# Third norm's centred values in the first tile's banks, its stages and GpSimd's first work in another order, first layer's weights in two transfers

## The reference

```
x = x + mamba_both_ways(layernorm(layernorm(x)))     # 8 passes: 4 sequences, forwards and backwards, 16 states
x = x + ffn_ref(layernorm(x), ...)                   # the transformer; this layernorm is "the third norm"

ffn_ref(x): for i in range(6):
    x = attn_layer(shift_tokens(x), Wqkv[i], q_scale[i], k_scale[i], Wo[i]) + x     # 16 heads of 64, window 32
    x = ffn_layer(shift_tokens(x), ln_g[i], ln_b[i], W1[i], b1[i], W2[i], b2[i]) + x
layernorm(x) = (x - mean(x)) / sqrt(var(x) + 1e-5)   # over the 128 features
```

## Time and profile before

| | us |
|---|---|
| median of 3 runs | 3966.04 (3959.29 to 3967.46) |
| the profiled execution, its own time | 3973.11 |
| its span, first to last instruction | 3971.3 |
| PE busy in it | 3732.7 (94%) |
| DVE, POOL, ACT busy | 3320.7, 3235.6, 2912.0 |

### The profile page before, as it was taken

One profiled execution on the slowest core, in us unless ns is written; L12 is line 12 of the kernel. 1 busy time (PEld: TensorE's weight loads), 2 busy tenths in 40 slices (PEclk: granted clock), 3 DMA queues, 4 the chain that ended last, 5 costly groups with the idle time before them and its releaser, 6 DMA issues.

```text
span 3971.3 us, 110564 instructions
## 1 busy us (share of the span) xinstructions
PE 3732.7 (94%) x43392; PEld 2529.3 (64%) x43392; DVE 3320.7 (84%) x3407; ACT 2912.0 (73%) x6890; POOL 3235.6 (81%) x2370
## 2 busy tenths in 40 slices
PE   7999999997579999999999999999999999999997
PEld 2333333333267777777777777777777777777775
DVE  4999999999478887888878888788878888788885
ACT  6555545553268887888878888788878888788885
POOL 3888788888388888888888888888888888888883
PEclk8999998899789999999999999999999999999999
DMA  1222222222100000000000000000000000000001
GB/s 66 79 70 71 77 70 70 75 73 82 46 5 13 2 16 2 17 2 16 2 2 17 2 16 2 6 13 2 16 2 6 13 2 16 2 6 2 2 2 44
DMA packets 30703, 102.12 MB, mean 26 GB/s; under 512 B 4580, under 2 KB 6504, under 8 KB 29296
## 3 DMA queue, kind: packets, MB, share of 16 engines
q1 hardware_dynamic: 30192, 95.05, 7.0%
HBM read 90.32 MB, written 4.72 MB: 24 GB/s over the span
## 4 chain that ended last, share of the span: by engine, by line
PE 67%; issue 2%; ACT 1%; POOL 1%; DVE 0%; POOLq 0%; ACTq 0%; DVEq 0%
PE ps L1101 17%; PE ps L1029 13%; PE ps L1090 9%; PE ps L1040 8%; PE ps L1078 7%; PE ps L1126 5%; PE ps L1139 3%; PE ps L1063 1%; PE ps L1051 1%; PE ps L1108 1%; PE ps L1114 1%; ACT prob L1232 0%; PE ps L1011 0%; ACT mixed L1241 0%; POOL resid L1530 0%
## 5 line engine op out<-in xcount | busy, mean ns | idle before, releaser
L1508 POOL TENSOR_TENSOR resid<-resid,sq 128x1024 f32<-128x1024 f32 x384 | 910.3, 2376 | 3.9 <-DVE sq L1362 3.7
L626 POOL TENSOR_TENSOR read<-state,c_row 128x1024 f32<-128x1024 f32 x256 | 714.9, 2811 | 165.6 <-DVE state L588 85.7
L1530 POOL TENSOR_TENSOR resid<-resid,rnorm 128x1024 f32<-128x1024 f32 x384 | 725.0, 1904 | 18.1 <-POOL rnorm L1522 0.4
L1101 PE MATMUL ps<-mixed,w_vo 128*128 128x128 f32 x6144 | 720.2, 276 | 3.0 <-ACT mixed L1241 2.3
L1101 PEld LDWEIGHTS ps<-mixed,w_vo 128*128 128x128 f32 x6144 | 711.1, 192 | 13.0 <-issue 4.6
L1029 PE MATMUL ps<-w_qk,xs_parts 128*128 128x512 f32 x2304 | 640.3, 414 | 43.6 <-issue 18.7
L1232 ACT ACTIVATE prob<-ps,stat 128x64 f32<-128x64 f32 x3072 | 650.9, 383 | 0.3
L1362 DVE TENSOR_TENSOR sq<-ps,rope_l 128x1024 f32<-128x1024 f32 x384 | 462.5, 1205 | 104.7 <-ACT sq L1194 104.7
L393 PE MATMUL mamba_ps<-read,ident 128*128 128x512 f32 x1024 | 520.8, 652 | 14.8 <-POOL read L626 14.8
L1375 DVE TENSOR_TENSOR resid<-ps,rope_l 128x1024 f32<-128x1024 f32 x384 | 464.4, 1209 | 69.4 <-ACT sq L1194 62.3
L1029 PEld LDWEIGHTS ps<-w_qk,xs_parts 128*128 128x128 f32 x2304 | 415.8, 192 | 157.9 <-issue 81.7
(11 more groups left out here) (138 smaller groups left out, 5685.9 us busy)
## 6 DMA issues: line engine op xcount, KB each, us to landing
c_row<-c_rows SPq DMA_DIRECT2D x128, 512.0 KB, 3.6
w_stage<-w_qk_hbm SPq DMA_DIRECT2D x6, 1024.0 KB, 4.8
vo_stage<-w_v_hbm SPq DMA_DIRECT2D x6, 512.0 KB, 3.8
vo_stage<-w_o_hbm SPq DMA_DIRECT2D x6, 512.0 KB, 4.6
xn<-x_hbm SPq DMA_DIRECT2D x4, 512.0 KB, 7.0
kept<-resid SPq DMA_DIRECT2D x8, 256.0 KB, 4.5
resid<-kept SPq DMA_DIRECT2D x8, 256.0 KB, 4.4
out_hbm<-resid SPq DMA_DIRECT2D x8, 256.0 KB, 2.0
```

Of the source, the lines that this page charges most:

```text
L626: pool.tensor_tensor(read[:, h, g % 2, :], state[:, h, g % 2, :], c_row[:, g % C_AHEAD, :], ALU.mult).then_inc(done[f"rd{h}"], 1)
L1101: last = pe.matmul(bank[:, 0:P], w_vo[:, l % 2, head_at(place_h), :], mixed[:, odd, place_h, :], start=place_h == 0, stop=place_h == HEADS ...
L1508: pool.tensor_tensor(qk[:, tile % 2, cols], qk[:, tile % 2, cols], sq[:, 1 + part, :], ALU.add).then_inc(done[f"rotated{part}"], 1)
L1530: pool.tensor_tensor(heads, heads, norms, ALU.mult).then_inc(done[f"normed{part}"], 1)
```

## The change

Four things are altered.

The centred values leave the ring: chunks 0 to 3 go to banks 0 to 3, chunks 4 to 7 to banks 2 and 3 by turns (`in_bank`). Chunk c of 4 and more waits until `in_norm` of chunk c-2 is done. `project0` of tile 0 waits for chunks 0 and 1 to have left banks 0 and 1, `score` of tile 0 for all eight chunks.

The norm's stages have another order: chunks 4 to 7 come between the first two tiles' stages, and so do the folds. GpSimd makes both rotary tables first, and `low_qk1` after the first tile's `rest`.

PE and ACT no longer wait for DVE's constants at the block's start. GpSimd no longer waits for the small attention masks (`const_loaded`); the tables' transfer now counts on `scale_loaded`.

Each layer's queries' and keys' weights come in two transfers of 512 KB, one for each half, with a semaphore each.

The diff, cut to what does something:

```diff
--- before.py
+++ after.py
@@ -745,8 +745,7 @@
-TURN_READERS = {"in_centre": "in_norm", "in_variance": "in_log",
-                "head_turn0": "copy_heads0", "head_turn1": "copy_heads1", "head_turn2": "copy_heads2",
+TURN_READERS = {"in_variance": "in_rstd", "head_turn0": "copy_heads0", "head_turn1": "copy_heads1", "head_turn2": "copy_heads2",
...
-def staggered(*stages):
-
-    return [(name, i - behind) for i in range(CHUNKS + 1) for name, behind in stages if 0 <= i - behind < CHUNKS]
...
-    pe[0:0] = staggered(("in_centre", 0), ("in_variance", 1)) + [("fold0", 0), ("fold1", 0)]
-    act_in = staggered(("in_square", 0), ("in_log", 1), ("in_rstd", 1))
-    insert_after(act_in, ("in_rstd", 3), ("high_qk0", 0))
-    insert_after(act_in, ("in_rstd", 5), ("high_qk1", 0))
-    act[0:0] = act_in + [("copy_folded0", 0), ("copy_folded1", 0)]
-    dve[0:0] = [("in_norm", c) for c in range(CHUNKS)]
-    pool[0:0] = [("rope0", 0), ("low_qk0", 0), ("rope1", 0), ("low_qk1", 0)]
+    def norms(*stages):
+        return [(f"in_{name}", c) for name, c in stages]
+
+    pe[0:0] = norms(("centre", 0), ("centre", 1), ("variance", 0), ("centre", 2), ("variance", 1), ("centre", 3),
+                    ("variance", 2), ("variance", 3), ("centre", 4), ("centre", 5))
+    act[0:0] = norms(("square", 0), ("square", 1), ("log", 0), ("rstd", 0), ("square", 2), ("log", 1), ("rstd", 1), ("square", 3),
+                     ("log", 2), ("rstd", 2)) + [("high_qk0", 0)] + norms(("log", 3), ("rstd", 3)) + [("high_qk1", 0)]
+    dve[0:0] = norms(*[("norm", c) for c in range(4)])
+    insert_after(pe, ("project0", 0), *norms(("variance", 4), ("variance", 5)))
+    insert_after(pe, ("project1", 0), *norms(("centre", 6), ("centre", 7)))
+    insert_after(pe, ("project0", 1), *norms(("variance", 6), ("variance", 7)), ("fold0", 0), ("fold1", 0))
+    insert_after(act, ("round", 0), *norms(("square", 4), ("square", 5)))
+    insert_after(act, ("square0", 0), *norms(("log", 4), ("rstd", 4), ("log", 5), ("rstd", 5)))
+    insert_after(act, ("square1", 0), *norms(("square", 6), ("square", 7)))
+    insert_after(act, ("square0", 1), *norms(("log", 6), ("rstd", 6), ("log", 7), ("rstd", 7)), ("copy_folded0", 0), ("copy_folded1", 0))
+    insert_after(dve, ("squares0", 0), *norms(("norm", 4), ("norm", 5)))
+    insert_after(dve, ("squares0", 1), *norms(("norm", 6), ("norm", 7)))
+    pool[0:0] = [("rope0", 0), ("rope1", 0), ("low_qk0", 0)]
+    insert_after(pool, ("rest", 0), ("low_qk1", 0))
...
-    done |= {name: sem(name) for name in ("in_centre", "in_square", "in_variance", "in_log", "in_rstd")}
+    done |= {name: sem(name) for name in ("in_centre", "in_square", "in_variance", "in_rstd")}
-    names = """wqk_loaded wvo_loaded w1_loaded w2_loaded scale_loaded const_loaded const_set vo_folded vo_copied rope_ready partner_ready
+    wqk_loaded = [sem(f"wqk_loaded{part}") for part in range(2)]
...
+
+    def in_bank(chunk):
+
+        return ps[:, chunk if chunk < 4 else S + chunk % 2, :]
...
             def load_qk(l):
                 if l:
                     sp.wait_ge(w1_low, l)
-                sp.dma_start(w_stage[:, :], hbm["w_qk"][l]).then_inc(wqk_loaded, 16)
+                for part in range(2):
+                    cols = slice(part * INNER, (part + 1) * INNER)
+                    sp.dma_start(w_stage[:, cols], hbm["w_qk"][l][:, cols]).then_inc(wqk_loaded[part], 16)
...
             load_heads(0)
-            sp.dma_start(rope[:, :, :, :], hbm["rope"]).then_inc(const_loaded, 16)
+            sp.dma_start(rope[:, :, :, :], hbm["rope"]).then_inc(scale_loaded, 16)
             load_qk(0)
...
         @block.tensor
         def _(pe):
-            pe.wait_ge(const_set, CONSTS_SET)
-
             def in_centre(chunk):
-                bank = turn_free("in_centre", chunk)
-                pe.matmul(bank, centring[:, :], resid[:, chunk * BANK:(chunk + 1) * BANK], start=True, stop=True
+                if chunk >= 4:
+                    pe.wait_ge(x_ready, chunk - 1)
+                pe.matmul(in_bank(chunk), centring[:, :], resid[:, chunk * BANK:(chunk + 1) * BANK], start=True, stop=True
                           ).then_inc(done["in_centre"], 1)
...
-                elif last and last[0] == "in_centre":
-                    pe.wait_ge(x_ready, last[1] + 1)
...
+                elif last and last[0] == "in_variance":
+                    pe.wait_ge(done["in_rstd"], 2 * last[1] + 1)
...
@@ -1019,6 +1031,8 @@
                     after(pe, ("rest", tile))
                     if t == 0:
                         pe.wait_ge(wqk_low, 2 * l + part + 1)
+                    if tile == 0:
+                        pe.wait_ge(x_ready, 2)
...
-                    pe.wait_ge(const_loaded, 80)
+                    pe.wait_ge(const_loaded, 64)
+                    pe.wait_ge(x_ready, CHUNKS)
...
         @block.scalar
         def _(act):
-            act.wait_ge(const_set, CONSTS_SET)
             act.preload_act_table_set("natural_log_exp_and_others")
...
             def high_qk(part):
                 def stage(l):
                     cols = slice(part * INNER, (part + 1) * INNER)
-                    act.wait_ge(wqk_loaded, 16 * l + 16)
+                    act.wait_ge(wqk_loaded[part], 16 * l + 16)
...
             def in_square(chunk):
                 after(act, ("in_centre", chunk))
-                act.activation(in_work(chunk), turn_bank("in_centre", chunk), ACT.Square).then_inc(done["in_square"], 1)
+                act.activation(in_work(chunk), in_bank(chunk), ACT.Square).then_inc(done["in_square"], 1)
...
             def in_log(chunk):
                 after(act, ("in_variance", chunk))
                 act.activation(in_work(chunk), turn_bank("in_variance", chunk), ACT.Ln, bias=eps_col[:, 0:1]
-                               ).then_inc(done["in_log"], 1)
+                               ).then_inc(done["in_rstd"], 1)
...
             def in_rstd(chunk):
-                after(act, ("in_log", chunk))
+                act.wait_ge(done["in_rstd"], 2 * chunk + 1)
                 act.activation(in_work(chunk), in_work(chunk), ACT.Exp, scale=-0.5).then_inc(done["in_rstd"], 1)
...
             def in_norm(chunk):
-                after(dve, ("in_rstd", chunk))
+                dve.wait_ge(done["in_rstd"], 2 * chunk + 2)
                 low, high = halves_of(xa, chunk * BANK, BANK)
                 for to, rows_h, ready in ((low, slice(0, 64), x_low), (high, slice(64, 128), x_ready)):
-                    dve.tensor_tensor(to, turn_bank("in_centre", chunk)[rows_h], in_work(chunk)[rows_h], ALU.mult).then_inc(ready, 1)
+                    dve.tensor_tensor(to, in_bank(chunk)[rows_h], in_work(chunk)[rows_h], ALU.mult).then_inc(ready, 1)
...
         @block.gpsimd
         def _(pool):
-            pool.wait_ge(const_loaded, 80)
             pool.wait_ge(const_set, CONSTS_SET)
...
@@ -1472,7 +1485,7 @@
             def scaled_rope(part):
                 def stage(l):
 
-                    pool.wait_ge(scale_loaded, 16 * l + 16)
+                    pool.wait_ge(scale_loaded, 16 * l + 32)
```

More of the change, by code:

```diff
@@ L880, in transformer @@
             for _, which, name in order if which in (None, 0) and name != "add_ff"}
-    done |= {name: sem(name) for name in ("in_centre", "in_square", "in_variance", "in_log", "in_rstd")}
+    done |= {name: sem(name) for name in ("in_centre", "in_square", "in_variance", "in_rstd")}
     x_low, x_ready = sem("x_low"), sem("x_ready")
-    names = """wqk_loaded wvo_loaded w1_loaded w2_loaded scale_loaded const_loaded const_set vo_folded vo_copied rope_ready partner_ready
+    wqk_loaded = [sem(f"wqk_loaded{part}") for part in range(2)]
+    names = """wvo_loaded w1_loaded w2_loaded scale_loaded const_loaded const_set vo_folded vo_copied rope_ready partner_ready
         wqk_high wqk_low rs_log newton_step out_low w1_high w1_low resid_loaded
@@ L886, in transformer @@
     z = {n: sem(n) for n in names}
-    (wqk_loaded, wvo_loaded, w1_loaded, w2_loaded, scale_loaded, const_loaded, const_set, vo_folded, vo_copied, rope_ready, partner_ready,
+    (wvo_loaded, w1_loaded, w2_loaded, scale_loaded, const_loaded, const_set, vo_folded, vo_copied, rope_ready, partner_ready,
      wqk_high, wqk_low, rs_log, newton_step, out_low, w1_high, w1_low, resid_loaded,
```

## The result

The changed kernel took 3921.54 us, median of 4 runs (3917.52 to 3924.77), against 3966.22 for the kernel before: ratio 0.9894, 95% interval 0.9881 to 0.9907, 44.7 us won. A second set, with the unaltered kernel run again, gave 3920.37 (6 runs) against 3964.69: ratio 0.9889 (0.9871 to 0.9906), 44.3 us. The forecast was 3929 in 3920 to 3939.

A forecast was written before the change was run, and what follows sets the result against it. PE's work bounds nearly everywhere, but the block's start is a chain of waits between engines. Gains of 33.1 us at half clock and 44 at high were mixed to 37: 3966.04 - 37 = 3929, range 3920 to 3939.

The forecast's parts named there:

- Rival C: Pipeline's fill, held by something unseen, gives the shift back: 0 to 25 us arrive at the end, 3941 to 3966; chance 0.05.
- D: PE's clock does not return to the high level at tile 3; at 100 us the time is 3977; chance 0.02.
- The first projection: `project0` of tile 0 starts at 1047.5 at half clock, against 1085.02: 37.5 won; 1044.4, held by GpSimd, at full.
- To the second of tile 0: Step to `project1` of tile 0: 6.63 before, now two averages and the projection, 6.4; hidden, still 37.5 won.
- To the first of tile 1: Step to `project0` of tile 1: 7.63 before, 7.65 now, with two norms on DVE; still 37.5 won.
- To the second of tile 1: Step to `project1` of tile 1: 6.49 before, 10.9 now at half clock, 6.8 at high; 4.4 lost at half clock.
- a third of the way from 33.1 to 44: Mixture of clock levels up to tile 3, between the gains at half and high clock: 37 us won.
- Rival B: PE's clock at the high level all through: 44 us won, 3922; chance 0.17.
- The clock from tile 3 on: A sign that the forecast is right: a granted PE clock of 1.00 from tile 3 on.
- The split of the weights: Two pieces neither give nor cost before ACT's cast at 1041.8; bounds nothing below, 0.5 us above.
- The masks: GpSimd's tables start at 1036, at worst 1038.0; done 1044.4 or 1046.4, both under 1047.5: costs nothing at half clock.
- The folds: 3.4 of their 3.78 us stand in the step to `project1` of tile 1, where 4.4 us are lost.

The follow-up runs named there:

- folds later: Changed kernel with both folds on PE moved behind tile 1's first transpose and their ACT copies later: 3911.21 us in one run, 3923.87 (6 runs) when repeated.

## Why the prediction was right, and where it was off

- **What bounds, and where.** Right: the gain lies in the block's first 90 us, and the rest takes the same time. Rival C (given back) and D (slower) are out: 2812.0 and 2810.3 behind score 3.
- **The first projection.** I had 47.5 at half clock and 44.4 at full on the scale of before, 18.9 and 15.8 after the block's start; it was 14.3. Held by GpSimd, as I said for the high clock. Earlier than my bound since the table landed 6.0 into the block, not at my 7.4, and the clock did not fall at the start at all. On the scale of before that is 1042.9, just ahead of the 1044 to 1048.5 that I had given as a sign.
- **To the second of tile 0:** 6.4 to 6.6 forecast, 5.5 measured, all at the high clock. **To the first of tile 1:** 7.65 forecast, 7.4 measured: DVE's chain with the two norms in it, as worked out. **To the second of tile 1:** 10.9 at the low and 6.8 at the high clock forecast, 8.4 measured, with the clock low for its first 5.7 us.
- **The sum there:** 37 us forecast, 41.5 measured. The step that was mis-sized is "a third of the way from 33.1 to 44". Measured it is three quarters of the way. No run shows the third as such. PE was busy for 8.00 of the 13 us from 1033 to 1046 and the clock was 1.00 throughout; it fell at 1048, in the wait of 2.73 us. Rival B (44 us, 3922), which I gave 0.17, came nearest by the number, though not by its course: B has the high level all through, and it was low from 26.0 to 32.8 us into the block and again from 39.7. What the Trainium skill says (cited in the prediction from "TensorE: Matmul & The Clock Gate", "What's actually happening": that activity releases the clock) was the better guide for the first 26 of these 35.6 us, and the idle matmuls in the kernel before, at 1.00 where it had 0.50, agree with it.
- **The clock from tile 3 on.** I had given 1.00 as a sign. It was 0.90 from 1075 us to score 3, where before had 1.00 from its tile 3's first projection (1124.90) to score 3. At that projection 42.5 us were won (96.3 against 53.8), at score 3 41.4, so 1 us was lost in between; rival D, which asked for 93 us at the low level, got 7.
- **The split of the weights.** Called 0, with bounds nothing below and 0.5 above. Wrong: without it ACT's cast waits 2.35 us. I had set the cast at 1041.8 on the half clock and forgot to ask again at the high one, where it comes 5.5 us earlier.
- **The masks.** By the prediction the wait is worth nothing at half clock and 2.0 us at full (GpSimd done at 1046.4 or at 1044.4; the 1.3 of the expectation above is not in its sum); measured 4.9 at the first projection. Of that, 1.4 is the table, there at 6.0 and not at 7.4, and 1.6 the masks, there at 11.0 where the kernel before had them at 9.4. They stand behind the weights on the queue in both, in the changed kernel behind two transfers and not one; whether that delays them is not shown.
- **The folds.** Forecast 4.4 us lost at the step in which they stood; measured 2.0 (8.45 less 6.49). Projection and averages ran at the low level as I had them; the folds (2.10) and the transpose ran at the high one. Moving the folds won nothing that can be told.
- **The median.** 44.7 and 44.3 us in the two sets against 43.1 and 40.4 between the block's start and the end in the traces (2942.7 less 2899.6, less 2902.3). The difference would be the first block, whose end scatters over 15 us with the same code. So the median's 3921.54 meets rival B's 3922 partly by chance, and it lies 1.5 us inside the lower end of my range: that the forecast held is owed to the width of the range as well. Why the first block's end scatters, and whether the change moved it at all, stays open: there is one trace of before.

## What to carry to other kernels

Where a stretch is bound by a chain of waits, price it at both levels of PE's clock, and ask anew at the high one for each transfer that was hidden at the low one. Give each stage of a chain its own buffers before touching the order, then let the next phase's work into the gaps: here the first, with the dropped waits, was worth 21.8 us and the second 19.7 more. Compare from a fixed point in the program, not from the launch, when the effect is smaller than the scatter of the part ahead of it, and repeat a single run before crediting an edit with what the clock gave.

## What was not expected of the hardware

- 32 more matmul instructions and as many weight loads on PE, doing nothing and done in a few us, cost 30 us later in the program, 16 cost 15 (one trace each), nearly all behind tile 83 of 192; part of it shows as waits for issue ahead of 32- and 64-column matmuls. The idle matmuls that raised the clock in the kernel before won 11.3 us so and lost 39.
- The clock's falls are not fixed by the code. In both traces of the changed kernel an idle stretch of 2.73 us on PE saw the level fall to 1.2 GHz for nearly 7 us; with three idle matmuls in it the level stayed at 2.4 GHz, but so it did in one trace with the same stretch unfilled. Two traces of one kernel (folds later) have 7 and 20 us at the low level up to score 3.
- A 1 MB transfer and its halves: the first half was there at 7.7 us into the block, when ACT asked for it; in the kernel with one transfer the whole came at 10.2.
